# Projecting q and k of a tile one step sooner, with their running sums moved to another place in VectorE's order

## What is computed

```python
q = sigmoid(heads(Wq, bq)); k = sigmoid(heads(Wk, bk)); v = heads(Wv, bv)
sink_in = normal / sum_d((q + EPS) * (cumsum(k) + EPS))
src_out = normal / sum_d((k + EPS) * (cumsum(q) + EPS))
cons_sink = sum_d((q + EPS) * (cumsum(k * src_out) + EPS)) / normal
cons_src = exp(clip(sum_d((k + EPS) * (cumsum(q * sink_in) + EPS)) / normal, -1, 1))
src_comp = cons_src / cumsum(cons_src) * normal
vs = v * src_comp
kv = cumsum(outer(k, vs))                      # 8 x 8 numbers a head and token
x = (q * sink_in / normal) . kv * sigmoid(cons_sink)
h = layernorm(inputs + x @ Wo + bo); h = layernorm(h + gelu(h @ W1 + b1) @ W2 + b2)
x2 = layernorm(inputs + h)
# then per token: the two best of 8 experts, relu(x2 @ wi + bi + x2 @ A_e @ B_e) @ wo + bo,
# weighted, a residual and a last layernorm
```

## Time and profile before

| | |
|---|---|
| median of 3 runs | 401.84 us (401.17 to 402.3) |
| the profiled execution's own time | 401.26 us |
| its span in the trace | 399.5 us |
| granted TensorE clock over the span | 0.996 of full speed |
| TensorE busy | 366.7 us (92%), 2056 matmuls |
| VectorE busy | 331.9 us (83%), 799 instructions |
| GpSimd busy | 254.5 us (64%) |
| ScalarE busy | 211.3 us (53%) |

### The profile page before, as it was taken

How to read it: one execution, slowest core, us unless ns; L and a number is a source line. 1 busy time by engine, 2 the same in 40 slices (tenths; PEclk the granted TensorE clock), 3 DMA queues, 4 the chain that set the end, 5 groups by cost and what they waited for, 6 DMA issues and landing times. The chain is left out here.

```text
span 399.5 us, 6696 instructions
## 1 busy us (share of the span) xinstructions
PE 366.7 (92%) x2056; PEld 258.8 (65%) x2056; DVE 331.9 (83%) x799; ACT 211.3 (53%) x393; POOL 254.5 (64%) x431
## 2 busy tenths in 40 slices
PE   8987999988998999899999999899999997999992
PEld 3565666865657784786668675778478664955651
DVE  2789989988689879998899979997999989834643
ACT  3340048055752886258842885278734873286450
POOL 2023849895489548983798449963898469946131
PEclk9999999999999999999999999999999999999998
DMA  8309043207300018100640038000810054000000
GB/s 259 155 12 220 6 93 93 81 1 169 96 0 2 0 42 215 38 0 2 163 126 2 2 86 205 2 1 19 203 45 1 2 137 101 2 0 29 0 26 27
DMA packets 19875, 26.59 MB, mean 67 GB/s; under 512 B 1664, under 2 KB 9984, under 8 KB 19840
## 3 DMA queue, kind: packets, MB, share of 16 engines
q1 hardware_dynamic: 19696, 25.96, 25.3%
q10 hardware_dynamic: 144, 0.21, 0.2%
HBM read 7.29 MB, written 2.10 MB: 23 GB/s over the span
## 5 line engine op out<-in xcount | busy, mean ns | idle before, releaser
L1009 POOL TENSOR_TENSOR prod<-cum_kv,q_fac 128x512 f32<-128x512 f32 x64 | 92.4, 1461 | 20.2 <-DVE cum_kv L1241 14.7
L448 PEld LDWEIGHTS pO<-s_wor,prod 128*128 128x128 f32 x512 | 63.0, 191 | 23.2 <-issue 13.0
L448 PE MATMUL pO<-s_wor,prod 128*128 128x128 f32 x512 | 67.3, 278 | 7.1 <-POOL prod L1009 6.9
L1235 DVE TENSOR_TENSOR kv<-k,vb 128x512 f32<-128x512 f32 x64 | 54.3, 849 | 1.3 <-DMA vb<-vs 1.0
L996 POOL TENSOR_TENSOR var_eps<-mv,s_con 128x4 f32<-128x4 f32 x32 | 6.8, 213 | 60.2 <-DVE mv L1263 60.2
L1241 DVE TENSOR_TENSOR_SCAN cum_kv<-p_ones,cum_kv,kv 128x512 f32<-128x512 f32 x32 | 40.6, 1277 | 0.6
L1241 DVE TENSOR_TENSOR_SCAN cum_kv<-p_ones,kv 128x512 f32<-128x512 f32 x32 | 38.8, 1216 | 0.7
L467 PE MATMUL pG<-hT,s_ffn 128*128 128x512 f32 x64 | 31.0, 607 | 2.9 <-ACT hT L835 2.2
L570 PE MATMUL pY<-s_moe,gel 128*128 128x128 f32 x256 | 33.0, 276 | 0.0
L570 PEld LDWEIGHTS pY<-s_moe,gel 128*128 128x128 f32 x256 | 31.0, 192 | 2.9 <-issue 1.9
L999 POOL TENSOR_TENSOR rstd<-var_eps,s_con 128x4 f32<-128x4 f32 x32 | 32.5, 1017 | 0.0
(11 more groups left out here) (190 smaller groups left out, 819.7 us busy)
## 6 DMA issues: line engine op xcount, KB each, us to landing
vb<-vs SPq DMA_DIRECT2D x64, 256.0 KB, 4.6
xT<-x_t SPq DMA_DIRECT2D x8, 256.0 KB, 4.1
xt<-x SPq DMA_DIRECT2D x8, 256.0 KB, 5.2
out<-y SPq DMA_DIRECT2D x7, 256.0 KB, 2.3
s_moe<-moe_w SPq DMA_DIRECT2D x1, 836.0 KB, 9.8
s_wor<-wo_rep SPq DMA_DIRECT2D x1, 512.0 KB, 7.9
s_ffn<-ffn_w SPq DMA_DIRECT2D x1, 512.0 KB, 8.3
s_con<-consts SPq DMA_DIRECT2D x1, 502.0 KB, 4.7
```

What stands on the lines that cost most here:

```text
L448: mm = pe.matmul(pO3[:, s, :], prod[:, m % 4, s * P:(s + 1) * P], s_wor[:, m, :], start=False, stop=(m == DH - 1), skip_group_check=True)
L1009: pool.tensor_tensor(prod[:, m % 4, :], cum_kv[t.par][:, m, :], q_fac[t.par][:, :], ALU.mult).then_inc(prod_ready, 1)
L1235: dve.tensor_tensor(kv[:, m % 3, :], k[t.par][:, :], vb[:, m, :], ALU.mult).then_inc(kv_ready, 1)
```

## The change

Tiles 0 to 3 are treated as before. From tile 4 on:

- TensorE projects q and k of a tile n = s+2 in step s, behind `reduce_out(b, 2)` and in front of `x2_T(c)`. Before it did so for a = s+1 at the very start of step s. (For tile 3 the two stand at the end of `third_step`, which is the same place in the order as the start of step 2.) Also, `inter2(d, 2)` moves ahead of `reduce_out(b, 1)`.
- ScalarE takes them out between `x2T_out(c)` and `v_out(a)`; before, at the start of the step.
- VectorE's two running sums of n stand on either side of `values(a)`: cum_q before it, cum_k between the joining of tile d's moments and `moments(b, 1)`. Before, both stood between the last `cumulate_kv(b, 7)` and `second_relu(d, 2)`.
- `outer_product(a, 2)` moves ahead of `second_relu(c, 0)` and `second_relu(c, 1)`, directly behind `cumulate_kv(a, 1)`.
- The waits follow the banks: `project_q(n)` and `project_k(n)` wait for the factor and the values of tile n-2 and for q and k of tile n-1 to have been taken out; `project_v(a)` waits until q of a+1 is out of pA, and the first `head_sums(a)` until k of a+1 is out of pB.

```diff
--- before.py
+++ after.py
@@ -353,16 +353,22 @@
         def _(pe):
             def project_q(t):
                 pe.wait_ge(xT_loaded[t.par], 16 * (t.slot_uses + 1))
-                if t.n > 1:
+                if t.n in (2, 3):
                     pe.wait_ge(qfac_ready, t.n)
+                elif t.n > 3:
+                    pe.wait_ge(qfac_ready, t.n - 1)
+                    pe.wait_ge(q_ready, t.n)
                 if t.n == 3:
                     pe.wait_ge(hsum_ready, 1)
                 pe.matmul(q_bank(t)[:, :], att("wq"), xT[t.par][:, :], start=True, stop=True).then_inc(q_proj, 1)
 
             def project_k(t):
                 pe.wait_ge(xT_loaded[t.par], 16 * (t.slot_uses + 1))
-                if t.n > 1:
+                if t.n in (2, 3):
                     pe.wait_ge(vs_ready, t.n)
+                elif t.n > 3:
+                    pe.wait_ge(vs_ready, t.n - 1)
+                    pe.wait_ge(k_ready, t.n)
                 if t.n == 3:
                     pe.wait_ge(hsum_ready, 2)
                 pe.matmul(k_bank(t)[:, :], att("wk"), xT[t.par][:, :], start=True, stop=True).then_inc(k_proj, 1)
@@ -370,8 +376,12 @@
             def project_v(t):
                 if t.n == 1:
                     pe.wait_ge(v_ready, t.n)
-                elif t.n > 1:
+                elif t.n == 2:
                     pe.wait_ge(q_ready, t.n + 1)
+                elif 2 < t.n < TILES - 1:
+                    pe.wait_ge(q_ready, t.n + 2)
+                elif t.n == TILES - 1:
+                    pe.wait_ge(qfac_ready, t.n)
                 pe.matmul(v_bank(t)[:, :], att("wv"), xT[t.par][:, :], start=True, stop=True).then_inc(v_proj, 1)
 
             def head_sums(t, pair, of_q):
@@ -379,6 +389,10 @@
                 base = (SUMS_AT, CONS_AT)[pair]
                 wide_sum = s_att[:, W_ATT["headsum"][1] - P:W_ATT["headsum"][1]]
                 if of_q:
+                    if pair == 0 and 2 < t.n < TILES - 1:
+                        pe.wait_ge(k_ready, t.n + 2)
+                    elif pair == 0 and t.n == TILES - 1:
+                        pe.wait_ge(vs_ready, t.n)
                     pe.wait_ge((k_ready, ksrc_ready)[pair], t.n + 1)
                     pe.wait_ge((kq1_ready, kq2_ready)[pair], t.n + 1)
                 else:
@@ -687,6 +701,7 @@
                 ffn_out(b, 2); ffn_out(b, 3)
                 inter2(c, 0); inter2(c, 1)
                 reduce_out(a, 0)
+                project_q(a.plus(1)); project_k(a.plus(1))
 
             def closing(c):
 
@@ -729,11 +744,12 @@
 
                 a, b, c, d = s.plus(1), s, s.plus(-1), s.plus(-2)
                 A, B, C, D = a.exists(), b.exists(), c.exists(), d.exists()
-                if A: project_q(a); project_k(a)
-                if D: inter_base(d, 2); inter1(d, 2); inter_base(d, 3); inter1(d, 3)
+                n = a.plus(1)
+                if D: inter_base(d, 2); inter1(d, 2); inter_base(d, 3); inter1(d, 3); inter2(d, 2)
                 if B: reduce_out(b, 1)
-                if D: inter2(d, 2); inter2(d, 3)
+                if D: inter2(d, 3)
                 if B: reduce_out(b, 2)
+                if n.exists(): project_q(n); project_k(n)
                 if C: x2_T(c)
                 if B: reduce_out(b, 3); reduce_out(b, 4)
                 if C: logits_and_lora(c)
@@ -932,6 +948,7 @@
                 udT_out(c); seed_x(a)
                 gated_constant(c)
                 normalise(b, 1)
+                q_out(a.plus(1)); k_out(a.plus(1))
 
             def closing(c):
 
@@ -960,9 +977,10 @@
 
                 a, b, c, d = s.plus(1), s, s.plus(-1), s.plus(-2)
                 A, B, C, D = a.exists(), b.exists(), c.exists(), d.exists()
-                if A: q_out(a); k_out(a)
+                n = a.plus(1)
                 if D: relu(d, 2); relu(d, 3)
                 if C: normalise(c, 2); x2T_out(c)
+                if n.exists(): q_out(n); k_out(n)
                 if A: v_out(a)
                 if C: gate_exp(c)
                 if A: spread_denominators(a, 0)
@@ -1495,7 +1513,7 @@
                 if B and b.n > 2: outer_product(b, 4); cumulate_kv(b, 3); cumulate_kv(b, 4); outer_product(b, 5)
                 if B: cumulate_kv(b, 5); outer_product(b, 6); cumulate_kv(b, 6); outer_product(b, 7)
                 if B: cumulate_kv(b, 7)
-                if A: cumulate_q(a); cumulate_k(a)
+                if A and a.n == 3: cumulate_q(a); cumulate_k(a)
                 if D: second_relu(d, 2); second_relu(d, 3)
                 if A: k_times_cum_q(a, 0)
                 if C: gate(c, 0)
@@ -1520,14 +1538,17 @@
                 if A: prefix_e(a)
                 if C: masked_lora(c, False)
                 if A: inverse_cum_e(a); source_factor(a); sink_factor(a)
+                n = a.plus(1)
                 if D: piece_moments(d, 3)
+                if n.exists(): cumulate_q(n)
                 if A: values(a)
                 if D: join_moments(d, 3)
+                if n.exists(): cumulate_k(n)
                 if B: moments(b, 1)
                 if A: query_factor(a); outer_product(a, 0); cumulate_kv(a, 0)
-                if A: outer_product(a, 1); cumulate_kv(a, 1)
+                if A: outer_product(a, 1); cumulate_kv(a, 1); outer_product(a, 2)
                 if C: second_relu(c, 0); second_relu(c, 1)
-                if A: outer_product(a, 2); outer_product(a, 3); cumulate_kv(a, 2)
+                if A: cumulate_kv(a, 2); outer_product(a, 3)
                 if B: moments(b, 2)
             opening(Tile(0))
             second_step(Tile(0))
```

## The result

The changed kernel takes 403.10 us (median of 8 runs, 402.37 to 403.58), the kernel before 401.90 (8 runs in the same session). One of these eight took 756.37 us and is left out of the ratio. The ratio is 1.0034 with a 95% interval of 1.0024 to 1.0044: slower by 1.2 us by the medians and by 0.34% by the ratio, just over the 0.3% that I had set as the bound. The profiled execution took 402.48 (span 400.7).

What follows compares the result with a forecast made beforehand. It took the loop through VectorE's last running sum to rden as the bound, the way over kq only 0.38 us longer than that over GpSimd and TensorE. Front gain against lateness: 4 x 0.2 = +0.8, giving 402.6, range 401.9 to 403.6.

Steps and rivals of the forecast that it cites:

- The front of a step: Last running sum to rden: two scans leave VectorE, gain 0.38 a step; rden then waits some 1.8 us for TensorE.
- The values: Scans around vs on VectorE: vs late by 0.26 or 0.15, q_fac by 0.58, first kv by 0.37.
- Piece 2's wait for its DMA: Third outer product, moved ahead of gel: its piece, issued behind the store of y, lands late; 0.38 of wait.
- The collision at piece 3: VectorE's piece 3 against a GpSimd product: too close to call; if second, it loses 1.1 and a step loses 0.4.
- piece 7 would then go free: VectorE's piece 7, if piece 3 is held: it meets no GpSimd product any more, 1.0 back.
- TensorE: Projections (1.72) fill the wait for x2 and cost nothing; up to 0.5 a step if that cover were gone.
- The end: Last interval, which only gets the reordered pieces: at most 0.3 either way.
- The sum: Four intervals from tile 3's rden to tile 7's, +0.2 each (+0.15 to +0.4): +0.8, median 402.6.
- (a): Rival: VectorE's holds by GpSimd products go away, 4 x 0.75 = -3.0, 398.9; chance 0.30.
- (b): Rival: one hold more, pieces 3 and 7 or two others; +1.2 a step, 406.6, or 404.2 in half; chance 0.18.
- (c): Rival: no difference, the overhang around the values equals the front's 0.38 or TensorE's order hides both; 401.8; chance 0.10.

Runs made afterwards that it cites:

- third product alone: The kernel before, with only outer_product(a, 2) moved ahead of the two second_relu: 404.12 us, ratio 1.0059.
- short scans: The kernel before, with the scans cum_q and cum_k of tiles 4 to 7 cut to one column: 399.38 us, ratio 0.9957.
- the projections alone: TensorE's and ScalarE's orders and the waits as changed, VectorE's order as in the kernel before: 401.23 us against 401.45, ratio 0.9994.
- store behind vb: The changed kernel, but SyncE issues the store of y behind pieces 2 and 3 of vb: 399.97 us, ratio 0.9965.
- the product of piece 5 giving way: Changed kernel, outer_product(a, 2) back behind the second_relu; GpSimd's product of piece 5 waits for VectorE's outer product of piece 7: 402.78 us, ratio 1.0033.
- the second product giving way: The changed kernel, but GpSimd's product of piece 1 waits for VectorE's outer product of piece 3: 401.88 us, ratio 1.0007.
- third product back: The changed kernel, with outer_product(a, 2) back behind the two second_relu: 399.79 us against 401.45 for the kernel before, ratio 0.9953.
- step 6 filled: Changed kernel, outer_product(a, 2) back behind the second_relu, plus two more pairs of TensorE matmuls in step 6's idle time: 400.07 us, ratio 0.9970.
- the last experiment: Changed kernel with outer_product(a, 2) back behind the second_relu, GpSimd's product of piece 5 waiting for VectorE's outer product of piece 7: 402.78 us.

## Why the prediction was nearly right, and what failed in it

The predicted 402.6 is 0.5 under the measured 403.1, and inside its own range of 401.9 to 403.6; the likeliest class was "within 0.3%", and it came out 0.04% outside. The mechanism was right in its parts. One choice between two cases went wrong and one term was left out.

- **The front of a step**: 0.38 predicted as all that two scans of 2.3 us together are worth, 0.44 measured (6.58 to 6.14), by moving them and by cutting them. The wait of 1.8 before rden came, the one for kq went. Right.
- **The values**: mis-sized. vs late by 0.26 or 0.15, q_fac by 0.58, the first kv by 0.37 were predicted; 0.17, 0.34 and 0.11 were measured in tile 5 (vs 0.07 in tile 4, where the wait had been 1.03). I took a scan put into a wait as 1.12 (1.20 less one overlap of 0.08). Where the engine would otherwise idle, both neighbours overlap: from the end of what stands before to the start of vs it adds 1.21 - 0.08 - 0.09 = 1.04, and 1.04 - 0.86 = 0.18. The second scan adds 1.02 into 0.80 in the same way.
- **Piece 2's wait for its DMA**: 0.38 predicted behind the store of y; 0.41 to 0.62 measured, and the store was the cause, since the order of SyncE alone removes it. The way of reasoning held (issue of the store, landing 3.2 later); the wait came out larger as VectorE arrived sooner. It costs 0.33 a step.
- **The collision at piece 3**: this is the step that failed, a choice between two cases. "Piece 3 may fall either way by parity" was why I took 0.2 a step between 0.15 and 0.4. It fell against VectorE in all five steps, odd and even, with 1.72 to 1.79, so the unfavourable end (0.4) was the whole case: 0.35, 0.33, 0.29 and 0.40 measured. I had the times within 0.2 (piece 3 at 26.25 predicted, 26.09 measured, from rden), but took the product's start of the earlier trace rows (26.35) as fixed. It came at 25.99, and not by chance: the reordering moves it. In tile 5 it starts at 25.86 to 26.03 from rden in the kernels with the third product ahead (unless it gives way), at 26.31 to 26.50 in those without it. What shortens is the two rows of additions that GpSimd does ahead of it: in tile 5 they take 1.70 or 1.71 and 2.58 or 2.59 in every kernel with two outer products behind the gel, and 2.14 or 2.15 and 1.68 or 1.69 in every kernel with one of them ahead, the reordering alone included. A margin of 0.1 that depends on both engines was read from one. That piece 7 would then go free was right; that piece 5 would be held in part (1.01 and 1.13) was missing.
- **What the trace shows of the mechanism**: the Trainium skill ("SBUF — State Buffer", section "SBUF: two separate sides") calls it an exclusive lock that the first to start holds for its whole instruction. The traces agree: the second one takes the rest of the first one's time and its own less about 0.12, be it kv behind a product (0.67 to 1.73) or a product behind kv (1.27 to 1.72). qk behind a product took 1.66 for 0.84. Every kv of 1.00 or more in the loops of the kernels before, changed, third product alone and short scans ends 0.54 or 0.55 behind the end of the product that held it, whether it had started 0.02 or 0.8 behind that product's start. Once piece 3 is second, its end therefore hangs on the product alone.
- **TensorE**: the projections cost nothing, x2 isn't waited for in the steps with projections, xT in none, and the wait for gel in front of the experts (0.81) is hidden. Right; the projections alone changed nothing.
- **The end**: a term put at nothing. I counted four intervals up to tile 7's rden and gave the stretch behind it "at most 0.3 either way". Tile 7's last sum is 0.61 late as well (37.25 to 37.86), and the span behind that rden is 0.57 longer.
- **The sum**: -0.44 at the front, +0.20 for values and the rest up to the end of the sums (store behind vb: 37.47 against 37.27), +0.33 for piece 2's wait, +0.20 for the holds' place: +0.29, as measured in that step. Four steps give 1.37 and the end 0.57: 1.94 by profiles. The medians say 1.2, with 1.0 to 1.8 in the interval. The whole profiles differ by 1.2 as well, since the changed one's opening was 0.74 shorter. The opening varies by more than that from one execution to the next (last section), and with it a stretch of half clock in it, so the mean granted clock sorts the executions. Of the kernel before, 43 of 71 executions in the later sessions have at most 0.992 and a median of 401.16, 28 have at least 0.994 and a median of 401.90. Of the changed kernel's eight, seven have at most 0.993 (median 402.81), one 0.997 (403.58). Like with like the difference is some 1.7, across sessions. So part of the nearness is luck: the prediction's 0.8 is held against 1.2, and the loss in steps and end is rather 1.7 to 1.9.
- **The rivals**: (a), the holds gone, wasn't had in the one way that was tried: the product of piece 5 giving way frees VectorE by 1.0 and the step gets longer by 0.68, as GpSimd's stretched products set the end. But its number, 398.9, was near what the kernel without the third product's move takes (399.8), for another reason. (b), pieces 3 and 7 both held in full, occurred nowhere; of its "or two others" the changed kernel has a part, piece 3 in full and piece 5 by 0.34 to 0.46, and GpSimd has then caught up. (c), no difference, is what the second product giving way does (1.0007): 0.53 late, 0.44 given back at the front.

The best complete version is the changed kernel with the third outer product left where it was: 399.79, 0.47% under the kernel before (0.34 to 0.61) and 0.8% under the changed one. Issuing the store behind pieces 2 and 3 instead gives 399.97, which can't be told from it.

## What to carry to other kernels

Split a step at the instruction where the engines meet (here the last running sum) and count what lies ahead of it and behind it apart: two scans of 2.3 us behind it were worth 0.44, and 0.6 of lateness ahead of it (third product alone) cost 0.6. Before an instruction that reads a DMA's result is moved up, look at what its DMA queues behind. And where two engines exclude each other in pairs of instructions, work out both starts for the changed order before leaving it to chance: the steps have nearly the same phase, so it mostly falls the same way in all of them (in the changed kernel in five of five; with short scans one step of four fell otherwise after 0.32 of waiting for a DMA). And freeing the one engine can cost the other more.

## What was not expected of the hardware

- An instruction put into a wait costs its duration less the overlap with both neighbours: 1.04 for a scan of 1.21.
- Three instructions in a row on two engines can hold each other in turn: in the last experiment product 7 starts 0.07 behind kq and takes 1.75, and qk, 0.63 behind that, takes 1.66.
- Executions differ in the opening: tile 3's rden starts anywhere from 130.28 to 131.68 over the profiles, 130.28 and 131.54 in two kernels that are alike up to there (third product back, step 6 filled). The first rden of all already varies, from 11.84 to 13.27. In seven of the thirteen profiles (first rden at 11.84 to 12.72) the granted clock is 0.50 (1.2 of 2.4 GHz) for a stretch between 35 and 41; in the six with a first rden at 12.74 or later it is 1.00 there. So starts are compared from an rden and not from the span's start, and the 0.74 by which the changed kernel's opening was shorter says nothing.
- After TensorE had idled for 2.21 or 2.22 us in step 6, the granted clock over the step was 0.96 in three of five profiles, and with the third product back sixteen matmuls took 2.80 instead of 1.95; in the eight profiles with 1.83 us and less it was 1.00 in this step.
- A kv that is held by a product ends 0.54 or 0.55 behind that product's end, wherever it started.
